# The values' bias of the third attention moves from the values to the residual X, and the values' products get the four result banks

## The reference, cut to what matters

```
q = einsum('bsd,ed->bse', image_emb, Wq) + bq      # image_emb = layernorm(x)
k = einsum('bsd,ed->bse', text_emb, Wk) + bk       # text_emb  = the context
v = einsum('bsd,ed->bse', text_emb, Wv) + bv
scores = einsum('bqd,bkd->bqk', q, k) * scale
probs = softmax(scores, axis=-1)
attended = einsum('bqk,bkd->bqd', probs, v)
x = x + attended
```

## Time and profile before

| | |
|---|---|
| median of 3 runs | 2507.31 us (2506.47 to 2512.39) |
| the profiled execution | 2501.06 us |
| its span | 2499.2 us |
| TensorE busy | 2270.4 us, 91% |
| VectorE busy | 1700.6 us, 68% |
| ScalarE busy | 1286.7 us, 51% |
| granted TensorE clock, mean | 0.926 of full |
| C2 in the span | about 1296 to 1561 us |
| of it the head, to the first score | about 1296 to 1352.4 us |

### The profile page before, as it was taken

How to read it: one execution, slowest core, us unless ns; L and a number is a source line. 1 busy time by engine, 2 the same in 40 slices (tenths; PEclk the granted TensorE clock), 3 DMA queues, 4 the chain that set the end, 5 groups by cost and what they waited for, 6 DMA issues and landing times. The chain is left out here.

```text
span 2499.2 us, 35652 instructions
## 1 busy us (share of the span) xinstructions
PE 2270.4 (91%) x13660; PEld 1198.8 (48%) x13660; DVE 1700.6 (68%) x3546; ACT 1286.7 (51%) x1732; POOL 157.0 (6%) x198
## 2 busy tenths in 40 slices
PE   8999999999567869999989999787999999999788
PEld 3333333333322356777665777563444444443387
DVE  4778877886579844352753453776799999997385
ACT  3555555564267721223532222640688777877753
POOL 1000000000035530000000000001000000000011
PEclk9999999998778878999989999895999999998898
DMA  3000000000131142210010211004301111010232
GB/s 134 5 5 9 10 10 5 10 10 10 47 138 61 57 158 82 77 36 1 13 47 17 74 58 50 7 17 98 65 16 17 31 18 30 2 35 2 78 124 70
DMA packets 63412, 108.48 MB, mean 43 GB/s; under 512 B 13402, under 2 KB 45031, under 8 KB 62215
## 3 DMA queue, kind: packets, MB, share of 16 engines
q1 hardware_dynamic: 61286, 101.48, 13.2%
q0 software_dynamic: 1536, 4.20, 0.5%
q10 hardware_dynamic: 418, 0.50, 0.1%
HBM read 87.88 MB, written 17.73 MB: 42 GB/s over the span
## 5 line engine op out<-in xcount | busy, mean ns | idle before, releaser
L2776 DVE TENSOR_REDUCE pm<-PS 128x1 f32<-128x512 f32 x768 | 473.0, 682 | 40.5 <-PE PS L2615 39.3
L2737 ACT ACTIVATE P<-PS 128x1024 f32<-128x1024 f32 (+1 forms) x416 | 422.4, 1024 | 119.4 <-PE PS L2653 116.8
L2615 PE MATMUL PS<-Ks,Qs 49*128 49x512 f32 x768 | 302.2, 480 | 19.5 <-DMA Qs<-q_parts 11.9
L2653 PE MATMUL PS<-Qs,Ks 51*128 51x512 f32 (+1 forms) x832 | 309.6, 459 | 0.4 <-ACT P L2737 0.4
L714 ACT ACTIVATE P<-PS 128x1024 f32<-128x1024 f32 (+1 forms) x208 | 213.3, 1026 | 170.7 <-PE PS L625 170.6
L2673 PE MATMUL PS<-P,V 128*17 128x256 f32 (+2 forms) x3072 | 261.3, 413 | 8.2 <-ACT P L2737 7.3
L638 PE MATMUL PS<-P,V 128*64 128x512 f32 (+1 forms) x832 | 227.2, 625 | 2.2 <-ACT P L714 2.2
L798 DVE TENSOR_TENSOR acc<-acc,P 128x1024 f32<-128x1024 f32 (+1 forms) x176 | 214.2, 1217 | 2.4 <-ACT P L714 0.2
L2653 PEld LDWEIGHTS PS<-Qs,Ks 51*128 51x128 f32 (+1 forms) x832 | 127.2, 185 | 171.3 <-issue 139.1
L2615 PEld LDWEIGHTS PS<-Ks,Qs 49*128 49x128 f32 x768 | 127.2, 194 | 54.3 <-DVE pm L2776 31.2
L1038 PE MATMUL PS<-ind,sel 128*8 128x512 bf16 (+3 forms) x288 | 82.6, 409 | 46.7 <-DVE ind L1145 24.0
(11 more groups left out here) (363 smaller groups left out, 4557.9 us busy)
## 6 DMA issues: line engine op xcount, KB each, us to landing
mi<-in_mask SPq DMA_DIRECT2D x32, 800.5 KB, 4.3
We<-in_L_ffn_w SPq DMA_DIRECT2D x16, 1024.0 KB, 7.3
Wg<-gate_rows SPq DMA_DIRECT2D x8, 1024.0 KB, 12.9
Qs<-q_parts SPq DMA_DIRECT2D x90, 64.0 KB, 3.4
R<-denominators SPq DMA_DIRECT2D x30, 128.0 KB, 2.9
Ks<-k_parts SPq DMA_DIRECT2D x18, 200.1 KB, 6.0
q_parts<-T SPq DMA_DIRECT2D x6, 512.0 KB, 2.7
k_parts<-Tk SPq DMA_DIRECT2D x6, 400.0 KB, 2.6
```

The costliest lines, as they stand in the source:

```text
L2615: m = e.matmul(PS[:, b, :], self.Qs[rows, s, pr, q0:q0 + 128], self.Ks[rows, s, pr, cs], start=True, stop=not masked)
L2653: m = e.matmul(ps, self.Ks[rows, s, pr, ks], self.Qs[rows, s, pr, q], start=True, stop=not masked)
L2737: e.activation(self.P[0:r, n % 4, :, :], PS[0:r, b:b + 2, :], ACT.Exp, scale=0.25).then_inc(*k.ac_exp.up((3, n)))
L2776: e.tensor_reduce(self.pm[:, u % 2, i, c:c + 1], PS[:, ring.of(("max", key)), :], AX.X, ALU.max).then_inc(*k.dv_max.up((3, *key)))
```

## The change

The one-row matmul of the bias goes from each value tile. The bias is now loaded as 128 equal rows, and VectorE adds it to each of the 16 tiles of X in the main part, four for each block, at the steps `score` of key tiles 3, 5, 7 and 9, behind the norm that reads the tile and ahead of the sum at the block's end. The value tiles of this layer get a ring of their own, the four result banks, which F1 must have left. And since the first `attend` writes those banks too, it waits for the last value tile to be read.

```diff
@@ KeysValues.__init__
-            self.bv = region.place("bv" + L, [1, D], F32)
+            self.bv = region.place("bv" + L, [128, D], F32)
...
+        self.value_ring = k.ring([2, 3, 6, 7]) if biased else ring
@@ KeysValues.sync
-            e.dma_start(self.bv[:], a[L + "bv"]).then_inc(*self.ld_b.up("all", 16))
+            e.dma_start(self.bv[:], a[L + "bv"].to_broadcast([128, D])).then_inc(*self.ld_b.up("all", 16))
@@ KeysValues.tensor, step "value"
-            b = self.ring.take(at, ("value", kt))
+            if self.biased:
+                at.wait_ge(*self.values_after)
+            b = self.value_ring.take(at, ("value", kt))
             at.wait_ge(self.ld, "all")
             for hf in range(2):
                 m = e.matmul(PS[0:r, b, 0:D], k.ctxT[:, hf, kt * 128:kt * 128 + r], self.wv[:, hf, :], start=hf == 0,
-                             stop=hf == 1 and not self.biased)
-            if self.biased:
-                at.wait_ge(self.ld_b, "all")
-                m = e.matmul(PS[0:r, b, 0:D], k.onesf[0:1, 0:r], self.bv[:], start=False, stop=True)
+                             stop=hf == 1)
@@ KeysValues.scalar, step "value"
-            e.activation(self.V[0:r, kt, 0:D], PS[0:r, self.ring.of(("value", kt)), 0:D], ACT.Copy).then_inc(
+            e.activation(self.V[0:r, kt, 0:D], PS[0:r, self.value_ring.of(("value", kt)), 0:D], ACT.Copy).then_inc(
                 *k.ac_proj.up((self.layer, "v", kt)))
-            self.ring.freed["value", kt] = (k.ac_proj, (self.layer, "v", kt))
+            self.value_ring.freed["value", kt] = (k.ac_proj, (self.layer, "v", kt))
@@ SingleAttention.tensor, step "attend"
             at.wait_ge(k.ac_exp, (layer, n))
+            if n == 0 and kv.biased:
+                at.wait_ge(k.ac_proj, (layer, "v", KT - 1))
@@ SingleAttention.vector
+        elif step == "score" and kv.biased and key[1] in (3, 5, 7, 9):
+            qb, kt = key
+            t = 4 * qb + (kt - 3) // 2
+            at.wait_ge(kv.ld_b, "all")
+            at.wait_ge(k.dv_xg, (self.norm, qb, 3))
+            at.wait_ge(k.dv_x, (*self.before, t))
+            e.tensor_tensor(k.X[:, t, :], k.X[:, t, :], kv.bv[:], ALU.add).then_inc(
+                *k.dv_misc.up(("X and bias", layer, t)))
@@ stages
+    kv2.values_after = (k.dv_x, ("F1", NT - 1))
```

More of the change, by code:

```diff
@@ L1583, in vector @@
                 at.wait_ge(k.dv_x, (*self.before, t))
+                if kv.biased:
+                    at.wait_ge(k.dv_misc, ("X and bias", layer, t))
                 e.scalar_tensor_tensor(out=k.X[:, t, :], in0=PS[:, (2, 3, 6, 7)[qt], 0:D],
```

## The result

| | before | after |
|---|---|---|
| median | 2509.06 us (10 runs, 2503.40 to 2520.40) | 2500.99 us (10 runs, 2496.51 to 2506.26) |
| profiled execution, its span | 2501.06, 2499.2 us | 2502.09, 2500.2 us |
| head of C2 in the profile, first key product to first score | 56.26 us | 48.52 us |

The ratio of the times is 0.9971, with a 95% interval of 0.9958 to 0.9984: 7.3 us less, between 4.0 and 10.5. The forecast was 10.9 less and 2496; the range, 2489 to 2504, held the time, and the sum was 3 to 4 us too good. A second comparison on another occasion gave 0.9961 [0.9939, 0.9983].

What follows compares the result with a forecast made beforehand. TensorE was taken to bound the kernel, busy for 91% of the span. Value tiles 11.5 plus first tile 1.1 minus bias load 1.7 gave 10.9 us less: 2507.31 to 2496, range 2489 to 2504.

Steps and rivals of the forecast that it cites:

- The bound: In the head, TensorE's list of work sets the time; a microsecond taken from the list is taken from the time.
- The value tiles: Head from the second value tile to the turn of the row values: 25.57 us becomes 14.0, 11.5 less.
- the turn covered: End of the value tiles: the last maximum and two tiles, 2.1 us, still cover the row values' 1.87 us.
- rival A: Value tiles: the gaps stay, a pair takes 1.6 us, gain 6.9 us, time 2500; chance 0.15.
- The first tile: Maximum and first value tile, no longer held for a bank: the second tile starts 1.1 us earlier.
- the bias load: Larger load ahead of ScalarE's first key: lands after 3.1 us, the key is 1.7 us later, cost 1.7.
- The bound on the slow side, 3.9: Bias load: costs 3.9 us if it lands only with the first megabyte of weights issued behind it.
- rival B: Head: new idle time ahead of the third key lowers TensorE's clock, load may land late; gain 5 to 9 us; chance 0.17.
- the main case: Whole kernel: the forecast itself, 10 to 13 us less; chance 0.55.
- The additions: Main part: VectorE's 16 additions of 0.42 us, 6.7 us in all, are hidden and cost 0.
- Rivals C and D: Behind the head, a transfer takes the gain back, 2507, chance 0.10; or half clock through the head, 2522, chance 0.03.
- the starting point: Whole kernel: the median of the runs shown before the change, 2507.31 us, from which 10.9 was taken.

Runs made afterwards that it cites:

- the eleven comparisons above: All eleven comparisons of changed versions with the kernel before: each ratio's interval holds what the head gained or lost, from 4.8 us more to 14.5 less.

## Why the prediction was nearly right

**The bound was right.** A microsecond off TensorE's list in the head was a microsecond off the head, and the main part behind it stayed at 208.4 us.

**The value tiles were right**, 11.5 forecast and 11.53 measured, in the terms of the sum: pairs of 1.23 us, two tiles, and the turn covered. Of the bounds, rival A (gaps that stay, 1.6 us a pair) is out. Of the 11.53, 10.0 are the ten pairs and 1.5 the last two tiles. The 1.00 us of a pair can be shared out: 0.43 is the bias product, 0.39 the two switches, and the rest, 0.18, the ring's bank. The forecast had the parts right, but the four banks and the bias product aren't independent. From 2.23 the ring alone takes 0.18 (2.05), the bias alone 0.62 (1.61), and both together 1.00. Neither half moved the time measurably (0.9997 and 0.9993), though each took some 3.2 us from the head; the second of them also pays for the load.

**The first tile** came out a little better, 1.43 us instead of 1.1. The path was as told; the clock was at half there in both kernels.

**The step that failed is the bias load**: "I take 3.1: the first key is 1.7 us later", and "Cost: 1.7". It cost 5.2 against the kernel before, and 6.1 by the run that takes the wait away. Two things were wrong with it. The landing was taken from loads with no large load issued behind them. This one is followed by 2 MB within a microsecond, and lands after 4.4 us; alone it takes 2.9 (the weights held back), and the term would have been right. The bound on the slow side, 3.9, knew the cause, and held the 3.12 that the key lost. And a row that contradicts the 3.1 was there: the kernel before has a second load of the very kind of L2310, at its start,

```profile
L513 SPq DMA_DIRECT2D bo<-in_L_xattn_bo x1: 1972/1972/1972, 11.2 to 11.2; - x1
...
DMA to landing us min/median/max: 3.1/5.6/8.0
```

and with more loads issued behind it and the DMA engines busy throughout (share 1.06 from 11 to 13 us) that one landed after 8.0 us.

The second is the clock. It was put into rival B, at 0.17, with "against it: the new gap stands alone, between two keys and six". A gap of 4.37 us, with 2.9 us of keys between it and the 3.09 us of the drain, went with 0.50 over the next 5 us of keys, and that cost 2.1. The forecast priced the wait at its length; it costs its length and what the clock takes afterwards. So rival B came true in place, mechanism and about in size (its gain of 5 to 9 holds the 7.74), while the main case came true in the value tiles. The range held the time because it had room for this load and for the scatter, and not because the sum was right.

By the formula of the Trainium skill (DMA: Bandwidth & Descriptors, Anatomy of one DMA) the larger load should have cost 0.3 us more than the small one, which is an estimate for this queue, since the formula was fitted on the GpSimd path. Alone it took 2.9 us to land where the small one let the key go 1.41 us after its issue, 1.5 more: the measurement decides against it, and the rows of the kernel were the better guide, though not good enough with traffic behind.

**The additions** cost nothing, as told: the main part is 208.3 us with and without them. **Rivals C and D** are out: nothing behind the head took the gain back (the eleven comparisons above), and the clock was back at 0.96 from 1312, and its next fall, around the first value tile, is in the kernel before too.

**The time.** The head explains the ratio: 7.74 of 2509 us is 0.9969, measured 0.9971 and 0.9961. That the spans of the two profiles show the opposite sign is scatter of other stages. The predicted 2496 was 5.0 us too low: 3.2 are the head's, and 1.8 the starting point, 2507.31 from three runs where ten gave 2509.06. The prediction also reads the scatter too small. With the profiled execution the four times it had lie 11.3 us apart (2501.06 to 2512.39) and not 6, which is only their distance from the median, and the ten runs lie 17 apart.

## What to carry to other kernels

When a load grows, ask first who waits on its semaphore: the values' bias is needed some 55 us later, and it held up the first key only because three loads counted on one semaphore. Giving it its own brought nearly as much (6.1 us of the head) as the whole change as first made (7.7). Price a wait on the busiest engine at its length plus what the clock takes back afterwards (1.6 and 3.0 us here), and take a load's landing from a row that has the same traffic behind it. A one-row bias product in a list of full products costs its own time and nearly the same again in switches (0.43 and 0.39 us); and two remedies that feed the same engine must be priced together, since each uncovers what the other hid.

## What the runs showed of the hardware

- A load that is already issued is slowed by those issued behind it in the same queue: 128 KB as 128 rows of 1 KB landed after 2.9 us alone and after 4.2 to 5.3 us with 2 MB behind it, and the first of these megabytes took 4.8 to 5.0 us behind the small load or alone, and 6.7 to 7.5 behind the large one.
- The granted clock after an idle time of TensorE ahead of the third key: after 0.19 us, 1.23 and 1.24 (three traces) and 1.37 us it stayed at 1.00, after 2.88, 4.22, 4.37, 5.23 and 5.29 us it stood at 0.50 for the next 3 to 5 us of full work; in the other two traces it was at 0.50 already. But after the drain's 3.1 us ahead of the first key it stayed at 1.00 in ten of twelve traces, so these rows don't make a rule of the idle time alone.
- Going from products of 128 rows to one of one row and back took 0.39 us in a pair (2.05 against 1.66 us).
